# Fourth layer's attention: the vector engine collects the outputs before reciprocal and maximum

## The chip, the cores and the metric

The kernel runs on one NeuronCore of a Trainium2 chip. The metric is the device time of one execution in microseconds, taken as the median of several runs; less is better. Engines are called PE (matrix products), DVE (vector), ACT (scalar functions), POOL (GpSimd) and SP (DMA issue). Each works through its own instructions in order and is held by semaphores that other engines raise.

## What is computed

Four gated layers run one after the other on x of 4 x 512 tokens with 128 channels; each takes a layer norm, an attention-like branch and a feed-forward branch, and adds their product to x. The change touches one branch alone, the attention of the fourth layer:

```python
qkv = einsum('bsd,de->bse', x, qkv_weights)        # 16 heads of 8 channels each
a = einsum('aib,ajb->aij', q, k) / sqrt(8)
a = tril * a + NEG_INF * (1.0 - tril)              # causal
a = softmax(a, axis=-1)
heads = einsum('aij,ajb->aib', a, v)               # [batch * head, 512, 8] -> [batch, 512, 128]
```

## The kernel before, in words

`l3_attn_stage` (from L2117) handles the four sequences of the batch one after the other, in a loop on each engine. Heads are packed: the 128 channels form four lanes of 32 channels, and a lane holds four heads. Queries go in blocks of 32 (`QB`), so that four heads of 32 queries fill the 128 rows of a tile; `qz` holds the queries with the channels of the other heads of the lane set to zero. A **unit** n of `PairSoftmax` is one query block (n // 2) and two of the four lanes, so there are 32 units in a sequence, and unit n looks at 32 * (n // 2 + 1) keys, 32 at the start and 512 at the end. Two units, an even and an odd one, make up a block.

For each unit, PE makes the scores of both lanes into two PSUM banks (L266, and the causal mask by one more product, L274). DVE takes the negated row maximum (`maximum`, L325). ACT makes the exponentials and the row sums (`probabilities`, L365). DVE inverts the sums (`inverse_sum`, L330). POOL scales the probabilities (L388). PE turns them by transposes into PSUM (`pe_turn`, L293). DVE copies the turned block of one lane to SBUF and ACT the other (`copy_turned`, L338). PE multiplies with the values (`pe_pv`, L306) into the one bank `PV_BANK`; the four lanes of an even and an odd unit fill its 128 rows.

`collect` (L2173 to L2187) empties that bank after every odd unit: one DVE product of the bank with a 0/1 mask of the heads into `own` (L2178), which counts `collected`. After every fourth block it adds a DVE sum over heads from `own` into `oT` (L2185). `pe_pv` of the next even unit waits for `collected`, since it writes the same bank.

The order of work is written by hand, engine by engine. In step n:

```python
PE:   scores(n + 2), pv(n - 2), turn(n)
DVE:  copy_turned(n - 1), inverse_sum(n + 1), maximum(n + 2), collect(n - 3)
ACT:  probabilities(n + 2), copy_turned(n)
POOL: scaling of n
```

Collecting does something in the even steps n from 4 on only, where n - 3 is odd. The first and second layer's attention use the same class, but their collecting is done on ACT (`collector="act"`), so the two lines that are moved do nothing there.

Of the kernel before, what the change touches and what calls it, by code (L numbers as in the profile page):

```python
# [186 lines left out]
class PairSoftmax:  # L187
# [155 lines left out]
    def vector(self, dve, b):  # L343
        self.maximum(dve, b, 0)
        self.maximum(dve, b, 1)
        self.inverse_sum(dve, b, 0)
        for n in range(self.units + 3):
            if 1 <= n <= self.units:
                for h in range(2):
                    if self.copiers[h] == "dve":  # L350
                        self.copy_turned(dve, self.nc.vector.tensor_copy, b, n - 1, h)
            if n + 1 < self.units:
                self.inverse_sum(dve, b, n + 1)
            self.maximum(dve, b, n + 2)
            if n >= 3 and self.collector == "dve":
                self.collect(dve, b, n - 3)


    def probabilities(self, act, b, n):
# [2387 lines left out]
```

How the kernel before makes its waits and increments, by code:

```python
    def join(self):  # L72
        self.eng.wait_ge(self.sem, self.n)
# [42 lines left out]
        @block.sync  # L116
        def _(sp):
            sp.dma_start(g.x[:], g.x_in.rearrange("b (t p) d -> p (b t) d", p=P)).then_inc(landed, 16)
            sp.dma_start(g.ident[:], g.c["ident"]).then_inc(landed, 16)
            sp.dma_start(masks[:, 0:P], g.c["causal128"]).then_inc(landed, 16)
            sp.dma_start(masks[:, P:P + 8], g.c["causal8"]).then_inc(landed, 16)
            sp.wait_ge(landed, 64)
# [1 line left out]
        @block.vector  # L124
        def _(dve):
            dve.memset(g.neghalf[:], -0.5)
            dve.wait_ge(landed, 64)
            nc.vector.tensor_copy(g.identb[:], g.ident[:])
            nc.vector.tensor_copy(g.causal128[:], masks[:, 0:P])
            nc.vector.tensor_copy(g.causal8[:], masks[:, P:P + 8])
# [19 lines left out]
        @block.vector  # L150
        def _(dve):
            for n in range(NT):
                nc.vector.bn_stats(stats[:, n], g.x[:, n]).then_inc(stats_done, 1)
            for n in range(NT):
                dve.wait_ge(stats_done, n + 1)
                nc.vector.bn_aggr(mv[:, n], stats[:, n]).then_inc(mean_done, 1)
            dve.wait_ge(mean_done, NT)
            nc.vector.tensor_scalar(mv[:, :, 1], mv[:, :, 1], LN_EPS, None, ALU.add).then_inc(var_ready, 1)
            dve.wait_ge(rstd_ready, 1)
            for n in range(NT):
                nc.vector.tensor_scalar(g.xn[:, n], g.x[:, n], mv[:, n, 0:1], rstd[:, n:n + 1],
                                        ALU.subtract, ALU.mult).then_inc(xn_ready, 1)
```

## Time and profile before

| | |
|---|---|
| median of 3 runs | 5366.92 us (5365.64 to 5392.56) |
| the profiled execution, its own time | 5376.71 us |
| its span, first to last instruction | 5374.9 us |
| busy shares of the span: PE, DVE, ACT, POOL | 80%, 64%, 49%, 44% |
| mean granted TensorE clock | 0.877 of full speed |
| the fourth layer's attention | from about 4610 to 5108 us of the span |

Busy shares are means over stages with different limits; what a change in one stage is worth is read from the waits of that stage. The line numbers are those of the kernel before. Matmul records are pipelined, so a block of matmuls begins some hundredths of a microsecond before the record of the block ahead of it ends.

### The profile page before, as it was taken

Reading aid. Unit: us, or ns where it says so; the run is one execution under the profiler, and the core shown is the slowest. Engines: PE = TensorE matmul, PEld = TensorE weight load, DVE = VectorE, ACT = ScalarE, POOL = GpSimd, SP = SyncE. Lnnn points to the kernel's source line nnn. Section 1 sums busy time; section 2 is a strip of 40 time slices with the busy share of each in tenths; the row PEclk is TensorE's granted clock in tenths of the full one; section 3 lists DMA queues with packets and bytes.
Section 4 is the critical chain, followed back from the end, with each engine's and each line's share of the span. In section 5 each row is a group of like instructions: output and inputs, shape, how many; then the busy total and the mean of one; then the engine's idle time right before and its main releaser. Section 6 shows DMA issues by size and latency. Waiting matters only on the chain. (4 is left out here: it accounts for less than half of the span.)

```text
span 5374.9 us, 89012 instructions
## 1 busy us (share of the span) xinstructions
PE 4317.4 (80%) x27516; PEld 3073.2 (57%) x27516; DVE 3450.0 (64%) x6519; ACT 2656.3 (49%) x7533; POOL 2357.6 (44%) x1611
## 2 busy tenths in 40 slices
PE   6888897888854437888888888888888888687788
PEld 4666564666521105666666666666666666355566
DVE  5555123555569987887787787877877886344412
ACT  3333343444233425666666666666666665234333
POOL 3443001333015556665566666655665664133300
PEclk8888998999965559999999999999999998567799
DMA  0000000000000001111111111111111110000000
GB/s 19 2 1 2 36 0 21 2 1 2 14 3 0 0 26 49 35 30 31 48 29 30 49 30 30 55 30 30 50 29 30 29 30 23 19 1 0 0 32 8
DMA packets 47561, 114.91 MB, mean 21 GB/s; under 512 B 16240, under 2 KB 22792, under 8 KB 46472
## 3 DMA queue, kind: packets, MB, share of 16 engines
q1 hardware_dynamic: 47112, 109.33, 7.5%
q8 instruction: 232, 3.80, 0.3%
q14 instruction: 217, 1.78, 0.1%
HBM read 34.85 MB, written 2.10 MB: 7 GB/s over the span
## 5 line engine op out<-in xcount | busy, mean ns | idle before, releaser
L2049 ACT ACTIVATE l2f_p<-ps,l2f_negmax 128x96 f32<-128x96 f32 x1536 | 503.6, 340 | 401.9 <-DVE l2f_negmax L1891 392.3
L1528 PE MATMUL ps<-l2f_wqkv,l2f_xsT 128*128 (+1 forms) x1152 | 580.4, 628 | 73.2 <-ACT l2f_xsT L2009 56.5
L1425 POOL TENSOR_TENSOR l2f_rn<-l2f_ss,neghalf 128x16 f32<-128x16 f32 x192 | 558.4, 2908 | 165.8 <-DVE l2f_ss L1859 165.8
L1431 POOL TENSOR_TENSOR l2f_cosd<-xnT,l2f_rot 128x1024 f32<-128x1024 f32 x192 | 521.6, 2717 | 149.8 <-DVE xnT L1866 149.8
L1875 DVE TENSOR_TENSOR xn<-xnT,l2f_rot 128x512 f32<-128x512 f32 x384 | 577.6, 1545 | 10.1
L1472 POOL TENSOR_TENSOR l2f_p<-l2f_p,l2f_rinv 128x384 f32<-128x384 f32 x384 | 317.6, 827 | 594.9 <-DVE l2f_rinv L1900 594.8
L1584 PE MATMUL ps<-l2f_pT,l2f_vw 96*128 96x128 f32 x3072 | 434.9, 286 | 15.4 <-DVE l2f_pT L1909 13.9
L1584 PEld LDWEIGHTS ps<-l2f_pT,l2f_vw 96*128 96x128 f32 x3072 | 391.5, 198 | 61.4 <-issue 51.9
L1558 PEld LDWEIGHTS ps<-l2f_kT,l2f_qz 128*128 128x128 f32 x3072 | 403.3, 196 | 11.8 <-issue 7.7
L1558 PE MATMUL ps<-l2f_kT,l2f_qz 128*128 128x96 f32 x3072 | 402.6, 275 | 0.0
L2065 ACT COPY l2f_oT<-ps 64x256 f32<-64x256 f32 x768 | 282.1, 367 | 174.9 <-PE ps L1584 160.9
L1528 PEld LDWEIGHTS ps<-l2f_wqkv,l2f_xsT 128*128 128x128 f32 x1152 | 204.2, 196 | 249.3 <-issue 191.8
L1909 DVE COPY l2f_pT<-ps 96x512 f32<-96x512 f32 x384 | 260.3, 678 | 99.6 <-PE ps L1570 94.4
L1866 DVE TENSOR_TENSOR xnT<-ps,l2f_rn 128x1024 f32<-128x1024 f32 x192 | 232.8, 1212 | 141.3 <-POOL l2f_rn L1425 141.1
L2049 ACT ACTIVATION_READ_ACCUMULATOR l2f_p<-ps,l2f_negmax 128x1 f32 x1536 | 312.1, 203 | 0.0
L388 POOL TENSOR_TENSOR l1a_p<-l1a_p,l1a_rinv 128x256 f32<-128x256 f32 (+3 forms) x128 | 160.4, 1254 | 327.2 <-DVE l1a_rinv L330 327.2
L1857 DVE TENSOR_REDUCE l2f_ss<-l2f_cosd 128x16 f32<-128x1024 f32 x192 | 234.2, 1220 | 90.8 <-ACT l2f_cosd L2015 60.0
L950 POOL TENSOR_TENSOR l2a_ysum<-l2a_ysum,l2a_hc 128x512 f32<-128x512 f32 x120 | 230.4, 1920 | 122.8 <-DVE l2a_hc L1106 121.6
L388 POOL TENSOR_TENSOR l3a_p<-l3a_p,l3a_rinv 128x64 f32<-128x64 f32 (+15 forms) x128 | 140.0, 1094 | 323.9 <-DVE l3a_rinv L330 323.9
L1594 PEld LDWEIGHTS ps<-l2f_wo,l2f_oT 128*128 128x128 f32 x1536 | 198.7, 204 | 105.5 <-issue 68.9
L1891 DVE TENSOR_REDUCE l2f_negmax<-ps 128x4 f32<-128x384 f32 x384 | 209.4, 545 | 68.8 <-PE ps L1558 66.2
L2031 ACT COPY l2f_qz<-ps 64x1024 f32<-64x1024 f32 x192 | 193.6, 1008 | 112.2 <-PE ps L1538 109.8
(352 smaller groups left out, 9856.8 us busy)
## 6 DMA issues: line engine op xcount, KB each, us to landing
l2f_vw<-l2f_vt SPq DMA_DIRECT2D x96, 384.0 KB, 4.1
l2f_vw<-l2f_vt SPq DMA_DIRECT2D x96, 256.0 KB, 3.6
l2f_wqkv<-L_ffn_Wqkv_dram SPq DMA_DIRECT2D x18, 512.0 KB
l2f_vw<-l2f_vt SPq DMA_DIRECT2D x72, 128.0 KB, 2.3
l0f_w<-L_w_dram SPq DMA_DIRECT2D x2, 2304.0 KB
l3f_w<-L_w_dram SPq DMA_DIRECT2D x2, 2048.0 KB
l2f_wo<-L_ffn_Wo_dram SPq DMA_DIRECT2D x6, 512.0 KB
l2f_w<-L_ffn_W_dram SPq DMA_DIRECT2D x6, 344.0 KB
```

Source lines behind the costliest of these rows:

```text
L388: self.nc.gpsimd.tensor_tensor(self.p[:, n % 3, :, 0:nk], self.p[:, n % 3, :, 0:nk], self.rinv[:, n].unsqueeze(2).broadcast_to([P, 2, nk]) ...
L1425: nc.gpsimd.tensor_tensor(rn[:, k], ss[:, k], g.neghalf[:, 0:HEADS], ALU.pow).then_inc(rn_ready[k], 1)
L1431: nc.gpsimd.tensor_tensor(cosd[:, k].rearrange("p (h d) -> p h d", d=DH), nrm[:, k].rearrange("p (h d) -> p h d", d=DH), rot[:, it.odd, k, ...
L1472: nc.gpsimd.tensor_tensor(p[:, n % 2], p[:, n % 2], rinv[:, QUAD * n:QUAD * (n + 1)].unsqueeze(2).broadcast_to([P, QUAD, KW]), ALU.mult).t ...
L1528: ins = nc.tensor.matmul(g.ps[:, 2 * (k % 2) + hf], xsT[:, WINDOW + t * P:WINDOW + (t + 1) * P], wqkv[:, bass.ds(weight_slot(it), 1), k * ...
L1558: ins = nc.tensor.matmul(out[:, c * KW:(c + 1) * KW], qz[:, pair, t % 2, j].rearrange("p h q -> p (h q)"), kT[:, pair, w * QB:w * QB + KW] ...
L1584: ins = nc.tensor.matmul(g.ps[:, 6, c * P:(c + 1) * P], vw[:, (QBS * t + j) % (2 * QBS), pair * P:(pair + 1) * P], pT[:, n % 2, c], start= ...
L1857: ch.done(nc.vector.tensor_reduce(ss[:, k], heads(cosd[:, k]), AX_X, ALU.add))
L1875: ch.done(nc.vector.tensor_tensor(heads(swp[:, k])[:, :, to:to + 32], heads(nrm[:, k])[:, :, frm:frm + 32], rot[:, it.odd, k, 1, t, to:to ...
L1909: nc.vector.tensor_copy(pT[:, n % 2].rearrange("p c q -> p (c q)"), g.ps[0:KW, 5]).then_inc(pT_copied, 1)
L2049: ins = nc.scalar.activation(p[:, n % 2, c], g.ps[:, 4, c * KW:(c + 1) * KW], ACT.Exp, bias=negmax[:, col:col + 1], accum_out=rowsum[:, co ...
L2065: nc.scalar.copy(oT[rows, quad * QUAD:(quad + 1) * QUAD, t % 2, j * QB:(j + 1) * QB], g.ps[rows, 6].rearrange("p (c h q) -> p c h q", h=2, ...
```

## The change

On DVE, in each step of `PairSoftmax.vector`, `collect` goes from the last place of the step to the place behind the copy of the turned block, ahead of `inverse_sum` and `maximum`. No instruction is added or removed, and the other engines' programs are the same row for row.

```diff
@@ PairSoftmax.vector
                 for h in range(2):
                     if self.copiers[h] == "dve":
                         self.copy_turned(dve, self.nc.vector.tensor_copy, b, n - 1, h)
+            if n >= 3 and self.collector == "dve":
+                self.collect(dve, b, n - 3)
             if n + 1 < self.units:
                 self.inverse_sum(dve, b, n + 1)
             self.maximum(dve, b, n + 2)
-            if n >= 3 and self.collector == "dve":
-                self.collect(dve, b, n - 3)
```

DVE, an even step in the second half of a sequence, where the block is not the fourth of its group (`l3a_own` is what collecting writes, `l3a_rinv` the inverse sums, `l3a_negmax` the maximum, `l3a_pT` the copied turned block):

```order
 L338 COPY l3a_pT<-ps 128x384
-L330 RECIPROCAL l3a_rinv<-l3a_rowsum 128x2
-L324 REGISTER_ALU
-L325 TENSOR_REDUCE l3a_negmax<-ps 128x2
 L2178 TENSOR_TENSOR l3a_own<-ps,l3a_consts 128x128
+L330 RECIPROCAL l3a_rinv<-l3a_rowsum 128x2
+L324 REGISTER_ALU
+L325 TENSOR_REDUCE l3a_negmax<-ps 128x2
 L335 REGISTER_ALU
```

The product into `own` now comes right behind the copy, and the reciprocal and the maximum of later units come after it.

DVE, the even step that also sums over heads into `l3a_oT`, which is every eighth step:

```order
 L338 COPY l3a_pT<-ps 128x512
-L330 RECIPROCAL l3a_rinv<-l3a_rowsum 128x2
-L324 REGISTER_ALU
-L325 TENSOR_REDUCE l3a_negmax<-ps 128x2
 L2178 TENSOR_TENSOR l3a_own<-ps,l3a_consts 128x128
 L2185 TENSOR_REDUCE l3a_oT<-l3a_own 128x128
+L330 RECIPROCAL l3a_rinv<-l3a_rowsum 128x2
+L324 REGISTER_ALU
+L325 TENSOR_REDUCE l3a_negmax<-ps 128x2
 L335 REGISTER_ALU
```

Here the sum moves along with the product, so both stand ahead of the reciprocal and the maximum.

## Rows read from the trace of the kernel before

**Rows 1.** Waits of PE in the stage: who waited for whom, total us, times, longest:
```profile
PE ps L306 <- DVE l3a_own L2178: 62.9, 52, 1.6
PE ps L266 <- DVE l3a_qz L2269: 15.7, 4, 5.9
PE ps L306 <- ACT l3a_pT L338: 7.7, 8, 1.3
PE ps L2248 <- DVE l3a_oT L2185: 6.1, 4, 1.5
```

**Rows 2.** Timeline, second sequence, late steps: start us, us, engine, line, operation [idle before]:
```profile
4841.43 0.59 ACT L338 COPY l3a_pT<-ps 128x512 f32<-128x512 f32 x1 [0.88 <-PE ps L293]
...
4841.83 1.68 POOL L388 TENSOR_TENSOR l3a_p<-l3a_p,l3a_rinv 128x896 f32<-128x896 f32 x1 [2.11 <-DVE l3a_rinv L330]
...
4843.76 0.69 DVE L338 COPY l3a_pT<-ps 128x512 f32<-128x512 f32 x1 [0.26 <-PE ps L293]
...
4844.77 0.58 ACT L338 COPY l3a_pT<-ps 128x512 f32<-128x512 f32 x1
4844.91 0.17 DVE L330 RECIPROCAL l3a_rinv<-l3a_rowsum 128x2 f32<-128x2 f32 x1 [0.46 <-ACT l3a_p L365]
4845.01 0.18 PE L274 MATMUL ps<-l3a_later,l3a_spread 32*128 32x32 bf16 x2
...
4845.24 1.16 DVE L325 TENSOR_REDUCE l3a_negmax<-ps 128x2 f32<-128x960 f32 x1 [0.16 <-PE ps L274]
4846.31 0.28 DVE L2178 TENSOR_TENSOR l3a_own<-ps,l3a_consts 128x128 f32<-128x128 f32 x1
...
4846.63 1.07 DVE L2185 TENSOR_REDUCE l3a_oT<-l3a_own 128x128 f32<-128x512 f32 x1
4846.74 1.07 PE L306 MATMUL ps<-l3a_pT,l3a_v 128*32 128x128 f32 x16 [1.55 <-DVE l3a_own L2178]
4847.74 1.09 PE L293 MATMUL ps<-ident,l3a_p 128*128 128x128 f32 x8
...
4848.76 1.08 PE L266 MATMUL ps<-l3a_kT,l3a_qz 32*128 32x256 f32 x8
4848.87 0.59 ACT L338 COPY l3a_pT<-ps 128x512 f32<-128x512 f32 x1 [1.04 <-PE ps L293]
...
4849.79 1.07 PE L306 MATMUL ps<-l3a_pT,l3a_v 128*32 128x128 f32 x16
...
4851.81 1.13 PE L266 MATMUL ps<-l3a_kT,l3a_qz 32*128 32x256 f32 x8
```

**Rows 3.** Groups of DVE instructions in the stage: count, busy us, mean ns, idle before:
```profile
L325 DVE TENSOR_REDUCE l3a_negmax<-ps 128x2 f32<-128x64 f32 (+15 forms) x128 | 92.4, 725 | 95.7 <-PE ps L274 94.2
...
L2178 DVE TENSOR_TENSOR l3a_own<-ps,l3a_consts 128x128 f32<-128x128 f32 x64 | 18.1, 282 | 7.2 <-PE ps L306 7.2
L2185 DVE TENSOR_REDUCE l3a_oT<-l3a_own 128x128 f32<-128x512 f32 x16 | 16.7, 1046 | 0.9
```

**Rows 4.** Stretches of 10 us, first and second sequence: busy by engine, then PEclk:
```profile
4710.00:4720.00 10.00, 8.53 (x53) 6.19 (x53) 3.17 (x7) 3.59 (x10) 3.15 (x2) 0.50 0.00 0
4800.00:4810.00 10.00, 7.65 (x45) 4.37 (x43) 3.73 (x9) 3.61 (x13) 2.64 (x3) 0.50 0.00 0
4830.00:4840.00 10.00, 7.10 (x82) 5.52 (x82) 5.61 (x11) 5.82 (x18) 4.62 (x4) 1.00 0.00 0
```

**Rows 5.** Timeline, the copy of v that opens each of the four sequences on DVE:
```profile
4624.24 0.68 DVE L2265 COPY l3a_v<-ps 128x512 f32<-128x512 f32 x1
...
4756.92 0.69 DVE L2265 COPY l3a_v<-ps 128x512 f32<-128x512 f32 x1 [2.08 <-PE ps L2238]
...
4872.97 0.69 DVE L2265 COPY l3a_v<-ps 128x512 f32<-128x512 f32 x1 [2.15 <-PE ps L2238]
...
4989.02 0.69 DVE L2265 COPY l3a_v<-ps 128x512 f32<-128x512 f32 x1 [2.15 <-PE ps L2238]
```

**Rows 6.** Timeline of PE, first sequence, 416 and 448 keys: value products that waited:
```profile
4707.23 1.50 PE L306 MATMUL ps<-l3a_pT,l3a_v 128*32 128x128 f32 x12 [1.41 <-DVE l3a_own L2178]
...
4718.11 1.50 PE L306 MATMUL ps<-l3a_pT,l3a_v 128*32 128x128 f32 x12 [1.48 <-DVE l3a_own L2178]
```

**Rows 7.** Timeline of PE, second sequence, the same two steps:
```profile
4832.91 0.85 PE L306 MATMUL ps<-l3a_pT,l3a_v 128*32 128x128 f32 x12 [1.42 <-DVE l3a_own L2178]
...
4839.52 0.85 PE L306 MATMUL ps<-l3a_pT,l3a_v 128*32 128x128 f32 x12 [1.48 <-DVE l3a_own L2178]
```

## The prediction

> **What bounds the kernel now.** The change lies in one stage, so I read the waits of that stage first, not the busy shares of the whole span. In the list of PE's waits [rows 1] the first entry stands apart: the value products (L306) wait 62.9 us for the collecting product on DVE (L2178), 52 times, 13 in each of four sequences. All that PE else waits for in the stage is far shorter, and most of it lies at the start or the end of a sequence. Next I read one such wait in order of time [rows 2]. It is step 26 of the second sequence. PE ends its scores with the mask product at 4845.01 + 0.18 = 4845.19. DVE takes the maximum of just these scores from 4845.24 to 4846.40, then the collecting product from 4846.31, and only then, at 4846.74, does PE begin the value product, after 1.55 us of idle time. The transposes follow it at once (4847.74), then the next scores (4848.76). In the odd step behind it there is no such wait: scores at 4848.76, values at 4849.79, the next scores at 4851.81, each begun as the one before ends. So PE bounds this stage, and the only time that it loses in the steady part is the wait for a collecting product that stands in DVE's queue behind a maximum which itself waits for PE's newest scores.
>
> **The change, part by part.** Nothing is added or removed; one product in each of 64 places and one sum over heads in each of 16 go ahead of a reciprocal and a maximum. No DMA and no queue of SP or POOL is touched.
>
> *The wait that goes.* What does the collecting product need? The values of unit n - 3, which PE makes ahead of the transposes of unit n - 1, and DVE's copy, the instruction in front of it, already waits for those transposes. So in its new place it starts as soon as the copy ends. In step 26 the copy of unit 25 ends at 4843.76 + 0.69 = 4844.45 [rows 2]; the product takes 0.28; its release reaches PE some 0.15 later (4846.31 + 0.28 = 4846.59 against a start at 4846.74). That makes 4844.88. In the odd step the values begin 0.11 after the mask product would (4849.79 stands 1.03 behind the scores' start at 4848.76); here that is 4845.01 + 0.11 = 4845.12. The release comes 0.24 earlier. So the whole wait goes: -62.9 us [rows 1].
>
> *What the product now delays.* Behind the copy, DVE sat idle for 0.46 us until ACT had its sums [rows 2]. The product of 0.28 fits in there: reciprocal and maximum start when they did. Cost taken: 0.
>
> *What the sum now delays.* In every fourth block the sum goes along: 0.28 + 0.04 + 1.07 = 1.39 us ahead of the reciprocal. The cover is 0.46 + 0.16 us of idle time, so that reciprocal and maximum come up to 1.39 - 0.62 = 0.8 us later [rows 2]. Who waits for them? POOL, then the transposes two steps on; and ACT, then the scores two units on. POOL's scaling of unit 26 ended at 4841.83 + 1.68 = 4843.51, the transposes that need it began at 4847.74; without the wait of 1.55 they begin at 4846.19, and 2.7 us are left. The exponentials of unit 28 were done before 4848.87, where ACT went on to its copy; the scores that need them began at 4851.81, so 2.9 us, and without the wait still 1.4. Both are over 0.8. The copies of unit 24 (ACT's ended at 4841.43 + 0.59 = 4842.02) have over 3 us to its values. Cost taken 0; the other end, all 16 sums on the path, is 16 x 0.8 = 12.8 us.
>
> *DVE as the next limit.* Two late units cost DVE 2 x (0.69 + 0.17 + 1.16) + 0.28 = 4.3 us, 5.4 with the sum, and cost PE, at the odd step's pace of 4851.81 - 4848.76 = 3.05 us, 6.1 us [rows 2]. DVE stays under PE.
>
> *The clock.* With 7.65 of 10 us busy PE ran at a granted 0.50 (1.2 GHz), and with 7.10 busy, half a sequence later, at 1.00 (2.4 GHz) [rows 4]. It rose within each sequence, but in the first one later: at 4710 to 4720 it was still 0.50. The first sequence took 4756.92 - 4624.24 = 132.7 us, the next two 116.05 each [rows 5], so a late rise costs 16.6. The change takes idle time out of both clock levels, and where in the sequence the clock rises may move either way. I take no gain and no loss; the rivals carry both ends.
>
> The sum against the profiled execution: 5376.7 - 62.9 + 0 = 5313.8. That execution lies 9.8 above the median of the runs shown, 5366.9, perhaps because its first sequence was slow [rows 5]; against the median the sum is 5304.0. I forecast the middle, **5309 us**, 1.1% under the median. A measurement of this kernel can tell about 0.5% from no change, 27 us: under 5340 is faster, over 5394 slower.
>
> **The rivals.** *The clock rises earlier.* With less idle time PE's clock may rise sooner. Two steps at 416 to 448 keys took 4718.11 - 4707.23 = 10.9 us at the low level [rows 6] and 4839.52 - 4832.91 = 6.6 at the high one [rows 7]. If it rises two such pairs earlier in four sequences, an estimate of some 3 us a pair (smaller units there) gives 4 x 2 x 3 = 24 us more: 5285. For it: the low level lasted into the steps with the largest waits. Against it: PE was busier at the low level than at the high one. The Trainium skill, TensorE: Matmul & The Clock Gate, Part 1, says that the default state is the throttled one and that activity releases it. By that rule this rival would be the likeliest; the trace agrees only in part, since the first and second sequence do the same work and differ.
>
> *The clock rises later.* The new pace may place the steps so that the clock rises late in more sequences, as it did in the first. Two more give 5309 + 33 = 5342, three 5359. For it: the one case in four [rows 5]. Against it: fewer gaps.
>
> *The bank stays the limit.* There is one bank for the values, and if the wait only changes its name (PE waiting for the copy, or for the product behind a late copy, for as long), the time stays at 5367, or 5377 as profiled. The point is the 0.24 us above: were DVE 1.8 us later at the copy, nothing would be won. The Trainium skill, Perfetto Trace Analysis, Optimization Strategy, says that the same gap repeating on the engine that should be saturated can mean too little SBUF or PSUM for the next tile. By that reading a second bank would be needed and the sum would be 0. The rows speak against it: the bank had been full since before 4843.76, the transposes that come behind it on PE having been done, and DVE did other work until 4846.31.
>
> *Slower.* DVE works in order, so the product and the sum hold up the reciprocal, then POOL, the transposes and PE. If PE's slack there were not the 2.7 us that I read but nothing, the gain would be lost to this new wait of the same length, and each collecting would come on top: 18.1 + 16.7 us of DVE time [rows 3], 5367 + 34.8 = 5402. It decides where the transposes' slack falls under 0.3 us. For it: maximum and reciprocal are what POOL and ACT wait for, and the maximum is DVE's largest group, 92.4 us [rows 3]. Against it: the slack of all three releases above.
>
> **How the numbers follow.** The forecast has 0.68, the earlier clock 0.15, the later clock 0.09 (half of it over 5340), the bank 0.05, slower 0.03. Faster by over 0.5%: 0.68 + 0.15 + 0.045 = 0.875, rounded to 0.88; within: 0.09; slower: 0.03. The range goes from 5285, the earlier clock, to 5338, which takes in the median's offset of 9.8, the 12.8 of the sums, and one late sequence; about 0.13 is left out.
>
> **What would show it.** Right: the entry of L306 waiting for L2178 falls from 62.9 to a few us; the waits of scores, transposes and values together do not rise by as much; each sequence at an unchanged clock is some 15.7 us shorter (62.9 / 4) between two copies of v. The product stands behind the copy, and the reciprocal still waits for ACT. Wrong: transposes (L293) that wait for POOL, or values that wait for L338 by a microsecond in each pair; then a step above on slack has failed. A time under 5290 or over 5330 with that wait gone would point to the clock, to be read from PEclk in the same stretches.

## The result, and the profile after

| | before | changed |
|---|---|---|
| median | 5373.45 us (4 runs, 5365.64 to 5392.56) | 5284.98 us (4 runs, 5280.07 to 5294.71) |
| the profiled execution, its own time | 5376.71 us | 5280.07 us |
| its span | 5374.9 us | 5278.3 us |

The ratio of the runs is 0.9839, with a 95% interval of 0.9814 to 0.9864: 88 us less, in the direction and at the place that were forecast, and on the lower bound of the range (5285). The forecast of 5309 us lies 64 us under this median of before; 24 us more came.

PE's waits in the stage of the changed kernel (who waited for whom, total us, times, longest), against [rows 1]:

```profile
PE ps L266 <- DVE l3a_qz L2269: 16.5, 4, 6.7
PE ps L2248 <- DVE l3a_oT L2185: 6.1, 4, 1.5
...
PE ps L306 <- DVE l3a_own L2178: 2.5, 4, 0.6
PE ps L306 <- ACT l3a_pT L338: 2.5, 4, 0.6
```

The wait of the value products for the collecting product is down from 62.9 us in 52 places to 2.5 us in four, one at the end of each sequence. The wait for ACT's copy of the turned block, 7.7 us before, fell along with it. Nothing grew in their place by more than 0.8 us (PE's wait for `qz`, 15.7 us before).

The same step as in [rows 2], in the first sequence of the changed kernel (start us, us, engine, line, operation, idle before):

```profile
4683.84 0.69 DVE L338 COPY l3a_pT<-ps 128x512 f32<-128x512 f32 x1 [0.26 <-PE ps L293]
...
4684.45 0.28 DVE L2178 TENSOR_TENSOR l3a_own<-ps,l3a_consts 128x128 f32<-128x128 f32 x1
...
4684.77 1.05 DVE L2185 TENSOR_REDUCE l3a_oT<-l3a_own 128x128 f32<-128x512 f32 x1
...
4685.09 0.18 PE L274 MATMUL ps<-l3a_later,l3a_spread 32*128 32x32 bf16 x2
4685.20 1.07 PE L306 MATMUL ps<-l3a_pT,l3a_v 128*32 128x128 f32 x16
4685.73 0.16 DVE L330 RECIPROCAL l3a_rinv<-l3a_rowsum 128x2 f32<-128x2 f32 x1
4685.81 1.14 DVE L325 TENSOR_REDUCE l3a_negmax<-ps 128x2 f32<-128x960 f32 x1
...
4686.20 1.09 PE L293 MATMUL ps<-ident,l3a_p 128*128 128x128 f32 x8
```

The product starts as the copy ends, and the values (L306) follow the mask product without idle time. With the product ending at 4684.45 + 0.28 = 4684.73 and some 0.15 us for its release, PE could have started at 4684.88; it started at 4685.20, so the margin is 0.32 us here. The sum does push the reciprocal and the maximum back, as was worked out, and no one is late for it.

Where the time went in the stage is read from four windows, one for each sequence, from DVE's copy of v to its copy of the result (length, PE busy, PEld, DVE, ACT, POOL busy, granted clock, then DMA). Before:

```profile
4624.20:4753.70 129.50, 105.68 (x716) 71.05 (x716) 52.53 (x123) 47.86 (x161) 38.20 (x34) 0.59 0.04 11
4757.00:4869.70 112.70, 88.97 (x716) 59.59 (x716) 52.79 (x122) 47.41 (x161) 38.21 (x34) 0.73 0.00 0
...
sum 467.70, PE 372.59 PEld 249.81 DVE 210.99 ACT 188.84 POOL 149.63; mean PE 93.15 PEld 62.45 DVE 52.75 ACT 47.21 POOL 37.41
```

Changed:

```profile
4610.10:4705.80 95.70, 88.26 (x716) 59.01 (x716) 52.75 (x123) 46.73 (x161) 38.19 (x34) 0.71 0.06 15
4710.60:4803.90 93.30, 85.93 (x716) 57.66 (x716) 52.75 (x122) 46.54 (x161) 38.19 (x34) 0.74 0.00 0
...
sum 382.60, PE 353.03 PEld 236.00 DVE 211.14 ACT 185.39 POOL 149.54; mean PE 88.26 PEld 59.00 DVE 52.79 ACT 46.35 POOL 37.38
```

PE's idle time in the four sequences is 467.7 - 372.6 = 95.1 us before and 382.6 - 353.0 = 29.6 us after: **65.5 us less idle**. PE's busy time, for the same 716 products in each sequence, is 372.6 against 353.0: **19.6 us less busy**. The granted clock differs with it, 0.59 against 0.71 in the first sequence. 17.4 of these are the first sequence alone (105.68 against 88.26). The stretches between the sequences took some 3 us more. That makes 82 us in the stage. Nearly all of the rest of the 96.6 us between the two profiled executions lies ahead of it: the stage's first copy of v came at 4624.24 us [rows 5] and comes at 4610.08 now, 14.2 us sooner, in code that the change does not touch.

### The profile page after: what moved, and what is told of

Read it like the earlier page. It is cut to its first block and busy times, and to the rows that moved or that the text cites. A ratio compares the mean times of both kernels' runs of the same rounds, so it can differ in the third digit from the quotient of the medians.

```text
span 5278.3 us, 89012 instructions
## 1 busy us (share of the span) xinstructions
PE 4284.7 (81%) x27516; PEld 3055.2 (58%) x27516; DVE 3449.7 (65%) x6519; ACT 2649.6 (50%) x7533; POOL 2356.5 (45%) x1611
## 5 line engine op out<-in xcount | busy, mean ns | idle before, releaser
L1538 PEld LDWEIGHTS ps<-ident,l2f_cosd 128*128 128x128 f32 x1536 | 182.5, 146 | 117.0 <-issue 116.6
```

## The experiments

Theory A: the gain is the wait that is gone, plus what the clock makes of the new pace. Rivals: the sum's new place costs something, the margin is wide, the bank is what matters, or the order on DVE is worth more than the wait. The measure in each is PE's idle time over the four sequences (length less busy, from the windows), because it hardly depends on the clock: in the three profiles of the kernel before it is 23.7 to 23.8 us in each of the 12 sequences, at granted clocks of 0.59 to 0.73.

| run | median, us | PE idle, us | PE busy, us |
|---|---|---|---|
| before | 5373.45 | 95.1 | 372.6 |
| changed | 5284.98 | 29.6 | 353.0 |
| changed again | 5292.7 | 29.5 | 348.8 |
| product alone moved | 5299.3 | 29.6 | 361.4 |
| between reciprocal and maximum | 5305.3 | 39.2 | 361.1 |
| order of before, two banks | 5289.2 | 24.4 | 366.7 |
| changed, products at the start | 5287.4 | 21.3 | 369.9 |
| before, products at the start | 5370.9 | 87.9 | 373.7 |
| changed, held clock, first try | 5272.2 | 18.0 | 337.8 |
| changed, held clock | 5252.2 | 13.9 | 328.0 |
| before, held clock | 5342.9 | 79.5 | 352.9 |
| before, second execution | 5394.4 | 95.1 | 396.2 |
| before, third execution | 5378.9 | 95.2 | 376.4 |

The last two are single executions. PE busy in the five runs with added products contains these products.

**The changed kernel again.** No edit.

> The changed kernel once more. Theory A (the wait of the value products for the collecting product is gone, 62.9 us; the rest of the gain is the timing of PE's clock in this stage and a spread of the earlier stages that has nothing to do with the change): 5280 to 5295 us, the wait of L306 for L2178 at 2.5 us again, while the time up to the start of the stage differs by some us from one execution to the next and the points where the clock rises may differ too. Theory B (all of the 88 us is the reordering itself): the same time, and the four sequences as long as in the first profile of the changed kernel, 100.5, 96.6, 102.6 us.

5292.7 us (5 runs, 5278.64 to 5303.15), against 5377.4 us of before with 10 runs on the same chip, ratio 0.9842 (0.982 to 0.9863). The wait for the collecting product is 2.5 us again, and the idle time is the same to 0.1 us. From one copy of v to the next the first three sequences take 100.6, 96.8 and 100.4 us, against the 100.5, 96.6 and 102.6 us that theory B had fixed. Only the third differs, by 2.2 us, which is too little to fell theory B alone. What speaks against it is that PE's busy time moves from one execution to the next with the same code: 353.0 and 348.8 us here, and far more in the kernel before, below.

**Only the product moves.**

```diff
-                self.collect(dve, b, n - 3)
+                self.collect(dve, b, n - 3, "product")
             if n + 1 < self.units:
                 self.inverse_sum(dve, b, n + 1)
             self.maximum(dve, b, n + 2)
+            if n >= 3 and self.collector == "dve":
+                self.collect(dve, b, n - 3, "sum")
```

> Only the collecting product stays ahead of reciprocal and maximum; the sum over heads (16 times 1.05 us) goes back behind the maximum. Theory A (the sum's delay of up to 0.8 us is covered): within 5 us of the changed kernel. Rival (the sum ahead of the reciprocal delays POOL and PE, up to 16 x 0.8 = 12.8 us): up to 13 us faster than the changed kernel.

5299.3 us (5282.97 to 5304.65); the idle time is 29.6 us, as with the whole move. So the sum's place costs PE no wait, the 12.8 us of the bound are 0, and all of the effect on the idle time is the product's. The median lies 6.6 us over the repeat, just outside the 5 us that were given, but the runs of the two overlap. Their profiled executions are 25.8 us apart: 12.7 of these are PE's busy time (361.4 against 348.8) and 14.0 the later start of the stage (4624.1 against 4610.1), so no wait.

**Collecting between reciprocal and maximum.**

```diff
-            if n >= 3 and self.collector == "dve":
-                self.collect(dve, b, n - 3)
             if n + 1 < self.units:
                 self.inverse_sum(dve, b, n + 1)
+            if n >= 3 and self.collector == "dve":
+                self.collect(dve, b, n - 3)
             self.maximum(dve, b, n + 2)
```

> Collecting stands between reciprocal and maximum. Theory A (the product must be done 0.24 us before PE ends its mask product, and the reciprocal's wait for ACT of some 0.5 us plus 0.17 us comes in front of it): the wait of L306 for L2178 comes back in part, 0.3 to 0.5 us in the steps at the high clock, 5 to 20 us in all, so 5290 to 5305 us. Rival (what mattered is that the product is ahead of the maximum, and the margin is wide): no wait comes back, the time of the changed kernel within 4 us. Rival (the reciprocal should not be held up): faster than the changed kernel.

5305.3 us, at the upper end of what theory A gave, 12.6 over the repeat of the changed kernel, and 9.6 us more idle time. A late step in the first sequence:

```profile
4707.12 0.17 DVE L330 RECIPROCAL l3a_rinv<-l3a_rowsum 128x2 f32<-128x2 f32 x1 [0.78 <-ACT l3a_p L365]
4707.29 0.29 DVE L2178 TENSOR_TENSOR l3a_own<-ps,l3a_consts 128x128 f32<-128x128 f32 x1
...
4707.72 1.07 PE L306 MATMUL ps<-l3a_pT,l3a_v 128*32 128x128 f32 x16 [0.60 <-DVE l3a_own L2178]
```

DVE waits 0.78 us for ACT in front of the reciprocal, and with the collecting product behind it the value product starts 0.60 us late. The wait for L2178 is 6.2 us in 15 places, 3.7 us more than in the changed kernel. The wait for ACT's copy is back too, 8.6 us in 12 places against 2.5 in four; why, no run shows. The margin is small, as predicted, and one instruction that itself waits for another engine uses it up.

**Two banks in the old order.** The value products alternate between two PSUM banks, of which one is taken from the turned blocks; the order on DVE is that of before.

```diff
-        pe.wait_ge(self.collected, self.at(b, n // self.every * self.every))
+        pe.wait_ge(self.collected, self.at(b, max(n // self.every * self.every - (self.TURN_BANKS == 2) * self.every, 0)))
...
+        return self.PV_BANK - (n // 2 % 2 if self.TURN_BANKS == 2 else 0)
...
+        at.TURN_BANKS = 2
```

> The order of the kernel before, with two PSUM banks for the value products, one taken from the turned blocks (two banks instead of three). Theory A (the gain is the wait that is gone, however it goes): the wait of L306 for L2178 goes and the time falls by 60 to 90 us as with the new order, 5280 to 5310 us, less what two banks for turned blocks cost in new waits of L293. Rival (the gain is in DVE's new order itself, earlier copies or reciprocals): the wait goes but the time stays within 20 us of before.

5289.2 us (5276.79 to 5302.6), ratio to before 0.9829 (0.9811 to 0.9847). PE no longer waits for L2178 at all; its idle time is 24.4 us. None of its sequences is over 98.9 us long. So the same gain comes without any change of order, and the rival by which the order on DVE has a worth of its own falls. Bank and order were two ways out of one wait, and the order is the one that needs no bank.

**Products without use at the start of a sequence**, in both kernels: 40 of 128 columns into an idle bank while PE waits for `qz`.

```diff
                 ins.then_inc(v_ready, 1)
+                for _ in range(40):
+                    nc.tensor.matmul(g.ps[:, 3, 0:P], g.identb[:], g.identb[:], start=True, stop=True)
```

> The changed kernel with 40 small products without use (128 columns, into a scores bank that is free) at the start of each sequence, in the 3.3 us in which PE waits for the masked queries. Clock theory (PE's clock stays at the high level through the early steps once it is there, and these are bound by PE at the low level): the granted clock reads 1.00 from the start of each sequence, and the stage is 30 to 60 us shorter than in the changed kernel, about 5235 us. Rival (the early steps are too thin to hold the high level): the clock falls at the first steps as before, and the time is within 8 us of the changed kernel.

> The kernel before with the same 40 products. If the clock holds in both, the two differ by the wait alone, and the distance between this and the one with the new order is what the wait costs at one clock: 55 to 65 us by theory A (62.9 us, a little less where the maximum is all that PE waits for). If the distance is 85 us or more, the new order is worth more than the wait, and theory A falls.

The clock theory missed here: the granted clock of the four sequences reads 0.70 to 0.71 and the median, 5287.4 us, lies with the changed kernel, as the rival had it, and not at 5235. The high level was not kept through the early steps. By the medians, the second question stays undecided: 5370.9 - 5287.4 = 83.5 us lies between the 55 to 65 us of theory A and the 85 at which it was to fall. The profiles decide it: those two executions are 5369.75 - 5302.95 = 66.8 us apart, with 87.9 - 21.3 = 66.6 us less idle time, 3.8 us less busy time and a stage that starts 3.4 us later. So the wait is what differs there; where the other 17 us between the medians lie, no trace shows.

**The clock held.** First try, four small products of 128 columns ahead of the scores of every unit of up to 352 keys as well:

> The products at the start, and four more of 128 columns in front of the scores of every unit of up to 352 keys. Clock theory: the high level is held through all steps; each unit costs about 0.25 us more of PE at the high level (22 units in 4 sequences, 22 us) against 2 us a pair saved in some 8 pairs a sequence: 5240 to 5270 us. Rival (early steps at the high level are bound by the chain over DVE, ACT and POOL, not by PE): the clock is high, but the stage gains under 20 us.

5272.2 us, just over the 5240 to 5270 us of the clock theory, which had the clock held in all four sequences. Two of them kept it, and they are 78.1 us long, the other two 100.6 and 99.0:

```profile
4614.90:4715.50 100.60, 94.32 (x804) 67.48 (x804) 52.86 (x123) 46.46 (x161) 38.17 (x34) 0.73 0.06 15
4724.00:4802.10 78.10, 74.42 (x844) 56.41 (x842) 52.45 (x121) 45.08 (x161) 38.17 (x34) 0.99 0.01 2
```

Then fewer and wider ones, in the new and in the old order:

```diff
+        if self.filler is not None and nk <= 352:
+            width = 512 if nk <= 96 else 256
+            nc.tensor.matmul(self.g.ps[:, 2 * (n % 2), 0:width], self.g.ident[:], self.filler[:, 0:width], start=True, stop=True)
...
+                for _ in range(5):
+                    nc.tensor.matmul(g.ps[:, 3], g.ident[:], xb[:], start=True, stop=True)
```

> The changed kernel with fewer and wider products without use: five of 512 columns at the start of each sequence, then one ahead of the scores of each unit of up to 352 keys (512 columns up to 96 keys, 256 beyond). Clock theory: as in the two sequences of the run before that kept the clock, a sequence takes about 78 us instead of 96, now in three or four of the four; PE's loop is shorter than with 40 small products, and its 5 us of waiting for instructions at the start of a sequence go; 5215 to 5245 us. Rival (whether the clock holds is chance): one or two sequences fall to the low level again and the time stays at 5255 to 5290 us.

> The same products without use in the kernel before. Where both kernels keep the high clock through a sequence, the difference of their lengths is what the wait costs with the clock out of play. Theory A: the 13 waits of a sequence, 10 to 16 us (less than 15.7 where at the high level something else than PE sets the pace), 40 to 64 us in all. Rival (most of the gain of the change came through the clock): under 8 us a sequence.

With the new order all four sequences run at a granted 1.00 and the median is 5252.2 us, ratio to before 0.9764 (0.9748 to 0.978): 40 us under the changed kernel as repeated. That is over the 5215 to 5245 us expected, for the added products take time of their own, 20.1 us of PE in the second sequence against 11.8 in the run before: a sequence is 85.6 us, not 78. With the old order it is 5342.9 us. The windows of the two, the new order first:

```profile
4710.30:4795.90 85.60, 82.66 (x770) 55.23 (x768) 53.72 (x121) 45.19 (x161) 38.17 (x34) 1.00 0.00 0
...
sum 341.80, PE 327.95 PEld 219.57 DVE 214.81 ACT 179.47 POOL 149.50; mean PE 81.99 PEld 54.89 DVE 53.70 ACT 44.87 POOL 37.38
```

```profile
4720.60:4826.10 105.50, 86.72 (x770) 57.84 (x768) 53.27 (x121) 46.81 (x161) 38.17 (x34) 0.97 0.00 0
...
4943.10:5058.80 115.70, 96.30 (x770) 64.49 (x768) 53.12 (x122) 45.74 (x160) 34.97 (x32) 0.87 0.00 0
sum 432.40, PE 352.90 PEld 235.17 DVE 213.18 ACT 185.94 POOL 149.52; mean PE 88.22 PEld 58.79 DVE 53.30 ACT 46.49 POOL 37.38
```

The idle time differs by 79.5 - 13.9 = 65.6 us, and the wait for the collecting product in the old order is 63.3 us. So in idle time the wait costs at the high level what it cost at both. The lengths, by which the expectation went, do not show the wait alone: a sequence of the old order is 18.9 to 30.1 us longer, over the 10 to 16 us of theory A, for the clock did not hold there. It reads 0.98, 0.97, 0.96 and 0.87, and PE's busy time is 24.9 us more.

**The kernel before, twice more.**

> The kernel before, profiled once more. Open is whether the late rise of the clock in its first sequence (129.4 us against 112.8 in the others) belongs to its pace or to one execution. If to its pace: the first sequence takes 129 us again. If to the execution: it takes 112 to 118 us here, and the stage is some 465 us long.

> The kernel before a third time. If the late rise belongs to its pace: the first sequence takes 129 us. If to the execution: some other length, and perhaps another sequence that is long.

Its sequences were 128.2, 121.0, 129.3 and 112.7 us long in the first of these executions, and 116.6, 129.4, 112.7 and 112.7 in the second. First and third sequence of the one that took 5394.4 us:

```profile
4615.40:4743.60 128.20, 104.47 (x716) 70.24 (x716) 52.44 (x122) 47.83 (x161) 38.21 (x34) 0.60 0.04 12
...
4874.30:5003.60 129.30, 105.51 (x716) 70.94 (x716) 52.45 (x122) 47.82 (x161) 38.21 (x34) 0.60 0.00 0
```

So a late rise is not bound to the first sequence, nor to one execution: in three profiles of the kernel before, 6 of 12 sequences are over 115 us long, all with more busy time at a lower granted clock, and with the same idle time. In three profiles of the new order (changed, again, product alone) the 12 sequences lie between 91 and 98 us, and none is late.

The traces show more than late rises. In each of the six long sequences the granted clock, once risen, fell back to 0.50 and rose again. One such fall, in the first sequence of the execution of 5394.4 us (a window, the value product that PE began next to its end, and the window behind it):

```profile
4709.00:4715.00 6.00, 5.37 (x59) 4.11 (x54) 3.29 (x6) 3.13 (x10) 2.34 (x2) 1.00 0.00 0
...
4715.92 1.17 PE L306 MATMUL ps<-l3a_pT,l3a_v 128*32 128x128 f32 x16 [1.55 <-DVE l3a_own L2178]
...
4717.00:4722.00 5.00, 5.00 (x32) 3.91 (x32) 1.80 (x3) 0.59 (x2) 1.79 (x1) 0.50 0.02 5
```

In the five profiles of the old order with one bank, with and without added products, there are 14 such falls more than 10 us into a sequence, each within some 1.5 us of the end of a wait of 1.35 to 1.62 us for the collecting product. In the 32 sequences of the eight runs where that wait is gone or at most 0.6 us, two banks in the old order among them, there is none. Most of the waits are not followed by a fall, so the wait alone does not say when one comes.

## Why the prediction was right, and where it was short

- **What bounds the stage**: right. PE is the bound, and the wait for L2178 was nearly all it lost in the steady part. Two stretches of the changed kernel (columns as above) show it at both clock levels, against [rows 4]:

```profile
4642.00:4652.00 10.00, 10.00 (x58) 5.78 (x54) 3.82 (x10) 4.23 (x15) 3.42 (x4) 0.50 0.01 2
4670.00:4680.00 10.00, 10.00 (x117) 7.77 (x114) 7.20 (x15) 6.52 (x20) 5.72 (x5) 1.00 0.01 2
```

- **The wait that goes, -62.9**: it was 60.4 (62.9 - 2.5), and 5.2 more from the wait for ACT's copy that shrank with it (7.7 - 2.5). Together 65.6, and the idle time fell by 65.5. The wait at ACT's copy was not in the sum; it was small.
- **What product and sum delay, 0 and 0 (end 12.8)**: right, shown by the run that moved the product alone.
- **The margin of 0.24 us**: measured 0.32 in the step shown, and put to the test by the run with the reciprocal in between, which lost 9.6 us, 3.7 of them to the collecting product.
- **The clock, "no gain and no loss"**: this is the term that was mis-sized. It gave 19.6 us in the two profiles compared, and by the medians some 20, an estimate (88 and 85 us, less the 65.5). The sign that was named for it came: a time under 5290 us with the wait gone. The rival of an earlier rise had the sign right. That its 5285 us, the bound of the range, is the time that came is luck: it counted on two pairs in each of four sequences, and sequences two to four gained almost nothing from the clock (PE busy 266.9 us before, 264.8 after). What went are the late rises, which I took for a feature of one sequence in one execution and priced at 16.6 us as a risk of the change, and the falls behind the wait, which I had not seen. They were a cost of the kernel before, in half of its sequences, and with two banks in the old order they were gone as well (PE busy 366.7 us, against 372.6 to 396.2 in the three profiles of before), so they go with the wait and not with the order on DVE.
- **The rule on the clock**: the Trainium skill, TensorE: Matmul & The Clock Gate, Part 1, has activity release the throttle. The trace agrees in that without the wait the clock no longer rose late, and that products without use kept it at a granted 1.00. One stretch does not fit: PE was busy 10.00 of 10 us and the granted clock stayed at 0.50.
- **The bank stays the limit**: wrong as a rival, for the wait went without a second bank; but the rule named beside it (the Trainium skill, Perfetto Trace Analysis, Optimization Strategy) pointed at a real alternative, since the run with two banks gained as much.
- **Slower**: among PE's waits in the changed kernel there is none of a transpose for POOL; the slack held.

What stays open: why the clock rises late and falls back in some sequences of the old pace and not in others, and whether the new pace excludes that or only makes it rarer. Twelve sequences of the new order without added products, and four with two banks, do not settle it.

## What to carry to other kernels

When an engine that bounds a stage waits for a small instruction, look at what stands in front of that instruction in its engine's queue: here 0.28 us of work was ready a microsecond and more before its turn, behind an instruction that itself waited for the waiting engine's newest result. Put what frees a buffer right behind the instruction that proves it ready, and ahead of every instruction that waits for someone else; even one such instruction in between cost 9.6 us of idle time. To judge such a change where PE's clock moves, compare idle time (length less busy) stage by stage: it came out at 65.5, 66.6 and 65.6 us in three pairs whose profiled executions were 97, 67 and 85 us apart, and whose medians 88, 84 and 91.

## What was not expected of the hardware

PE can be busy without a gap for 10 us and stay at a granted 0.50, as the stretch from 4642 to 4652 us shows, so a full engine was no sign of a high clock here. With products without use the granted clock read 1.00 through four sequences, and PE's busy time fell from 353 to 328 us although there were more products to run. Short products in large number seem to have a price of their own: with 40 of them at the start and four in each early unit, PE stood 4.89 us at the start of a sequence with no other engine to wait for.

```profile
4720.19 2.07 PE L2240 MATMUL ps<-l3a_xb,l3a_wq 128*128 128x512 f32 x2 [4.89 <-issue]
```

With the 40 at the start alone, or with five wide ones there and one in each early unit, that wait is not among the waits of PE; what makes it is not shown. And the stage's start moved from 4610 to 4624 us between executions of kernels whose earlier code is the same, as much as many a change is worth.
